# Attention scores issued as two pairs of heads, with V products and jobs between the pairs

## What is computed

```
xn = layernorm(x)
Q, K, V, U = silu(xn @ Wq), silu(xn @ Wk), silu(xn @ Wv), xn @ Wu      # 8 heads of 16
scores = (Q K^T + bias[relative position, head]) / sqrt(16), causal mask
weights = silu(scores)                                                 # no softmax
x = x + (weights @ V) * silu(U)
xn = layernorm(x)
gates = softmax over the top 2 of 8 logits (xn @ w_gate.T)
x = x + sum over e of gates[:, e] * ((xn @ w_in[e].T) @ w_out[e].T)
```

## Time and profile before

| | |
|---|---|
| median of 3 runs | 421.82 us (419.15 to 422.48) |
| profiled execution, first to last instruction (the only time shown of it) | 420.7 us |
| TensorE matmul busy | 368.3 us, 88% |
| DVE, ACT, POOL busy | 262.4, 244.1, 150.3 us |
| mean clock granted to TensorE | 0.885 of full speed |

### The profile page before, as it was taken

How to read it: one execution, slowest core, us unless ns; L and a number is a source line. 1 busy time by engine, 2 the same in 40 slices (tenths; PEclk the granted TensorE clock), 3 DMA queues, 4 the chain that set the end, 5 groups by cost and what they waited for, 6 DMA issues and landing times.

```text
span 420.7 us, 5792 instructions
## 1 busy us (share of the span) xinstructions
PE 368.3 (88%) x1708; PEld 155.3 (37%) x1708; DVE 262.4 (62%) x774; ACT 244.1 (58%) x485; POOL 150.3 (36%) x213
## 2 busy tenths in 40 slices
PE   0778869999999799999899899999999699998392
PEld 0433335455433333524333344432433243333151
DVE  3325730473887825868477539538999249568867
ACT  1426744788886557866466478845665467674013
POOL 5210220121208811446007534307527331443826
PEclk9996985999999958999569889959999779999877
DMA  4869583035602730272004700460005600000001
GB/s 76 278 212 266 161 222 95 19 101 168 158 2 57 208 87 0 62 212 54 26 2 128 197 26 0 147 179 2 26 1 170 156 26 0 2 2 25 1 0 50
DMA packets 34454, 37.89 MB, mean 90 GB/s; under 512 B 6256, under 2 KB 20080, under 8 KB 34424
## 3 DMA queue, kind: packets, MB, share of 16 engines
q1 hardware_dynamic: 34424, 37.53, 32.4%
HBM read 24.92 MB, written 12.60 MB: 89 GB/s over the span
## 4 chain that ended last, share of the span: by engine, by line
PE 59%; DMA 14%; DVE 12%; SPq 5%; POOL 4%; ACT 3%; issue 3%; DVEq 0%; POOLq 0%; ACTq 0%
PE score L555 19%; PE o_acc L571 13%; PE jobp L639 10%; DMA rows_dram<-k_hi 9%; PE jobp L599 5%; DVE score L804 4%; DMA k_stack<-rows_dram 4%; SPq L364 3%; PE jobp L594 3%; DVE xn L840 3%; ACT wts L699 2%; PE jobp L657 2%; POOL ymix L519 2%; PE jobp L632 2%; PE jobp L606 2%
## 5 line engine op out<-in xcount | busy, mean ns | idle before, releaser
L699 ACT ACTIVATE wts<-score,far 128x512 f32<-128x512 f32 (+3 forms) x384 | 201.6, 584 | 93.6 <-DVE score L804 63.4
L804 DVE TENSOR_TENSOR score<-score,bias_near 128x384 f32<-128x384 f32 (+2 forms) x320 | 128.0, 439 | 85.6 <-PE score L555 84.4
L555 PE MATMUL score<-q_stack,k_stack 64*128 64x512 f32 (+3 forms) x384 | 133.3, 469 | 22.8 <-DMA k_stack<-rows_dram 14.8
L555 PEld LDWEIGHTS score<-q_stack,k_stack 64*128 64x128 f32 x384 | 57.5, 199 | 166.5 <-issue 106.5
L519 POOL TENSOR_TENSOR ymix<-ymix 128x512 f32<-128x512 f32 (+2 forms) x84 | 69.0, 822 | 95.4 <-DVE ymix L910 90.9
L571 PE MATMUL o_acc<-wts,v_pad 128*32 128x512 f32 (+3 forms) x768 | 89.9, 543 | 1.0 <-ACT wts L699 1.0
L639 PE MATMUL jobp<-mm_e,xn2T 128*128 128x512 f32 x116 | 70.7, 702 | 0.9 <-DVE ymix L910 0.8
L910 DVE TENSOR_TENSOR ymix<-jobp,gates 128x512 f32<-128x512 f32 x56 | 38.0, 684 | 20.8 <-PE jobp L639 20.7
L594 PE MATMUL jobp<-ident,xn 128*128 128x128 f32 x64 | 13.8, 353 | 18.0 <-DVE xn L840 18.0
L840 DVE TENSOR_SCALAR xn<-xs,mv,rstd 128x128 f32<-128x128 f32 x64 | 28.0, 500 | 0.6 <-POOL rstd L458 0.4
L488 POOL TENSOR_TENSOR q_lo<-q,q_hi 128x512 fp32r<-128x512 f32 x7 | 9.7, 1393 | 50.9 <-DVE q_hi L850 50.9
(11 more groups left out here) (85 smaller groups left out, 265.4 us busy)
## 6 DMA issues: line engine op xcount, KB each, us to landing
q_stack<-rows_dram SPq DMA_DIRECT2D x64, 128.0 KB, 3.5
k_stack<-rows_dram SPq DMA_DIRECT2D x64, 128.0 KB, 3.2
rows_dram<-k_hi SPq DMA_DIRECT2D x16, 256.0 KB
xs<-in_L_attn_x SPq DMA_DIRECT2D x8, 256.0 KB, 5.3
win_s<-in_L_ffn_w_in SPq DMA_DIRECT2D x8, 256.0 KB, 2.9
wout_s<-in_L_ffn_w_out SPq DMA_DIRECT2D x8, 256.0 KB, 3.2
rows_dram<-q_hi SPq DMA_DIRECT2D x8, 256.0 KB
rows_dram<-q_lo SPq DMA_DIRECT2D x8, 256.0 KB
```

The costliest lines, as they stand in the source:

```text
L555: pe.matmul(score[j][:, 0:n], k_stack[rows, b % 2, h // 2, kb * P:(kb + 1) * P], q_stack[rows, half, h // 2, q0 - half * HALF:q0 - half * ...
L699: act.activation(wts[:, number % 2, j, 0:n], score[j][:, 0:n], ACT.Silu, bias=far[:, h:h + 1], scale=HD ** -0.5).then_inc(weighed[j], 1)
L804: dve.tensor_tensor(score[j][:, 0:near], score[j][:, 0:near], bias_near[:, 4 * quad + j, c0:c0 + near], ALU.add).then_inc(biased[j], 1)
```

## The change

TensorE now issues S0 and S1 of group i+1, then V of group i−1, then all jobs of slot i, then S2 and S3. Behind those stand S0 and S1 of group i+2, from the next slot. ACT does all jobs of slot i−1 between weigh 1 and weigh 2. DVE does add 0 and add 1 of group i+1, then the side jobs of slot i−1, then drains all banked jobs of slot i, then add 2 and add 3. A banked job that stood second in its slot is thus drained by DVE one slot sooner. No operation is added or removed, and the plan, the buffers and the waits are the same.

```diff
+def bank_jobs(jobs):
+    return [j for j in jobs if j[0] in BANKED]
+
+def side_jobs(jobs):
+    return [j for j in jobs if j[0] not in BANKED]
...
 # TensorE
                 if group and after:
                     scores(after, 0)
+                    scores(after, 1)
                 if before:
                     times_v(before)
-                if group and after:
-                    scores(after, 1)
-                for job in first_job(jobs):
+                for job in jobs:
                     job_pe(job)
                 if group and after:
                     scores(after, 2)
-                for job in later_jobs(jobs):
-                    job_pe(job)
-                if group and after:
                     scores(after, 3)
...
 # ScalarE
                 if group:
                     weigh(group, 0)
-                if i > 0 and TIMELINE[i - 1][0]:
-                    for job in first_job(TIMELINE[i - 1][1]):
-                        job_act(job)
-                if group:
                     weigh(group, 1)
                 if i > 0 and TIMELINE[i - 1][0]:
-                    for job in later_jobs(TIMELINE[i - 1][1]):
+                    for job in TIMELINE[i - 1][1]:
                         job_act(job)
                 if group:
                     weigh(group, 2)
...
 # VectorE
                 if not group:
                     if before:
-                        for job in later_jobs(TIMELINE[i - 1][1]):
+                        for job in side_jobs(TIMELINE[i - 1][1]):
                             job_dve(job)
                         copy_outputs(before)
...
                 if after:
                     add_bias(after, 0)
+                    add_bias(after, 1)
                 if group and before:
-                    for job in later_jobs(TIMELINE[i - 1][1]):
+                    for job in side_jobs(TIMELINE[i - 1][1]):
                         job_dve(job)
-                if after:
-                    add_bias(after, 1)
                 if group:
-                    for job in first_job(jobs):
+                    for job in bank_jobs(jobs):
                         job_dve(job)
                 if after:
                     add_bias(after, 2)
```

## The result

The changed kernel takes 394.81 us (median of 4 runs, 392.04 to 397.37), the kernel before 422.15 us (4 runs, 419.15 to 425.09): ratio 0.9423, 95% interval 0.9292 to 0.9554. Medians are of all runs and ratios of fast runs alone, so a ratio can differ by a per cent from the quotient of two medians. The forecast was 407, range 396 to 422 from a median of 421.8. The time moved the way that was forecast, by 27 us (24 by the ratio) instead of 15.

The account below looks back on a forecast made before the run. TensorE was taken to bound five stretches of 280.3 us, with 140.4 us fixed. Span 420.7 − 32.1 (TensorE) + 7.7 (loop) + 9.8 (DVE) = 406.1, so 407 us; range 396 to 422.

Parts of the forecast that it names:

- TensorE's slot: Full-clock slots of two banked jobs: four scores together at 0.66 and touching jobs save 0.73 us each, 16.1 over 22.
- second count, by mode changes: Two-job slots on TensorE: three tiling-mode changes instead of six at 0.22 us each give 0.66 instead of 0.73.
- Two-job slots at half clock: Ten slots of two banked jobs at half clock gain 1.0 us each on TensorE, 10 us.
- One-job slots: Twenty slots with one job of about 1 us go from 3.14 to 2.80, gaining 0.3 each, 6 us.
- The loop of V behind S1: V queued behind S1 makes a loop of 2.80 us, costing 5.0 in slots without banked job, 2.7 with short ones.
- DVE's side jobs: Side jobs on DVE between add 1 and the drains cost 9.8 us: 6.3 for nine norms, 3.5 for 35 others.
- The sum: Whole span: 420.7 − 32.1 + 7.7 + 9.8 = 406.1 us, so a time of 407; forecast case 403 to 413, chance 0.45.
- DVE hides all: Rival: DVE's side jobs cost nothing, 9.8 us less, 397 us (396 to 403); chance 0.17.
- The clock rival: Rival: 15 us more at half clock behind DMA waits, or four scores costing 0.99: 413 to 421 us; chance 0.24.
- The slower rival: Rival: side jobs make DVE last, delaying drains, adds 2 and 3 and four weighs: 432 us (426 and more); chance 0.14.
- ACT's move: ACT's jobs moved to one place between weigh 1 and weigh 2: hidden under V's 0.99, up to 0.3 us showing with V of 128 columns.
- DMA stretches: Four stretches of DRAM write and stack reload stay near 17 us each, 66.8 in all, with longer waits for the stack.

Follow-up runs that it names:

- the pairs apart: Changed kernel with TensorE's later jobs moved behind S2 and S3, and DVE draining them behind add 3: 396.97 us against 424.69.
- the spare buffer: Changed kernel with a third wts buffer for heads 0 and 1: 383.93 us against 420.12, ratio 0.9205.
- the warm version: Changed kernel with 4 idle matmuls ahead of S0 of the second unit in batches 1 to 3: 385.96 us against 423.45, ratio 0.9134.

## Why the prediction was right, and its size not

- **TensorE's slot.** Right: four scores at 0.66, jobs at 0.96, 3.57 for 3.65. In the 19 two-job slots at full clock in both profiles the gain is 0.71 us each, V to V, for 0.73; the 22 and 22 of the table give 14.5 us for 16.1. Touching jobs were taken at 0.10 less and give 0.21 (2.12 to 1.91). The prediction's second count, by mode changes, came out at 0.66 because it left out that a lone score now runs beside another. An estimate from the rows here: a second pair of scores adds 0.23 (0.66 less 0.43) and a second touching job 0.86 (1.91 less 1.05), so about 0.20 is left each time (0.43 less 0.23, 1.05 less 0.86) for the change to the next kind of work. With V, scores and jobs as the kinds, the FF slot has six such changes before, five with the pairs apart and three now. One change and one lone score less are 0.20 + 0.23 = 0.43, two more changes less are 0.40; measured were 0.42 and 0.39. One price per change thus covers both the places of the scores and the jobs that touch.
- **Two-job slots at half clock.** Mis-sized: 10 us, and by the table 30.3 less 14.5 is 15.8. They were priced as if the half-clock parts stayed; of the eight slots at half or part half clock before, three are at full clock after, and three others have fallen, so this row mixes the order with the clock.
- **One-job slots.** Mis-sized: 6 us of gain, measured a loss of 1.0. The term took the 3.14 us of a 512-query slot with a full job for all; the 18 took 2.84 before already, which is the new loop's 2.80.
- **The loop of V behind S1.** Right in kind (more waiting for V, 1.19 from V to weigh 0), too large in size: 5.0 us for slots without a job (3.3 measured) and 2.7 for short jobs (0.7). Of the 3.3 us only 0.8 lies in the eight slots at full clock in both profiles (2.21 to 2.31); 2.5 us lie in four slots that one profile has at half clock.
- **DVE's side jobs.** The term that failed most: 9.8 us of cost (its own numbers give 0.8 a norm, not 0.7). In two-job slots none of it is seen (0.82 us gained with side jobs, 0.65 without); elsewhere it was not measured by itself. DVE has less slack, though: its wait for scores fell from 84.4 to 51.6 us, and its adds have 6% of the chain instead of 4%.
- **The sum.** The case that came is the rival "DVE hides all", 397, which had 0.17, and not the forecast's own 403 to 413. That the sum without DVE's term, 397.4, is so near the 397.5 is in part luck: the two-job slots gave 4 us more than the sum has, one-job slots 7 less, the loop cost 4 less, and the DMA stretches gave 2.6 that it has at nothing.
- **The clock rival.** It had the wrong sign. It held that longer waits for the DMA would bring 15 us more at half clock; there were 19 us less in the means, worth 6 to 7 of the 27 us. It also read all four parts at half clock behind the DMA waits as over 10 us; the one behind the third is 6.8. Why the clock stays up better with the new order is not settled. Among the versions with TensorE's new order and no idle matmuls, those in which TensorE is idle less have less half clock: its short idle times (up to 1.5 us) sum in the traces to 29.9 us with its order alone, 25.1 with ACT's, 20.1 with DVE's, 13.0 in the changed kernel and 11.6 with the spare buffer, with 108, 99, 94, 81 and 61 us at half clock. The kernel before doesn't fit in: 7.6 us idle, and 101 at half clock.
- **The slower rival.** What it described, four weighs late together, was not seen: ACT's wait for the adds fell from 63.4 to 54.9 us. A case that was missed lies beside it: without the orders of ACT and DVE, TensorE's new order gives no gain that shows. The prediction put ACT's move at nothing, but without it the rest is −8.1 instead of −19.9.
- **DMA stretches.** Right: 16.1 to 16.7 us, with waits of 21.3 us for 14.8. Ahead of the low halves at 125.72 us in the chain stand DVE's adds and the high halves now, no longer POOL's sums.

## What to carry to other kernels

Matmuls of one tiling should stand together. Here a place cost 0.43 us with one or two scores of 512 columns and 0.66 with three or four, at full clock, so that each change from one kind of work to another is worth about 0.20 us (an estimate from these rows). When work is regrouped on one engine, the engines that feed and drain it must cut their queues at the same points, or what one gains the others take back. And where one program alone varies by 7% with the clock, compare the cost of the same slots at full clock, and the time at half clock apart from it, before believing a difference of a few us.

## What was not expected of the hardware

- With idle matmuls in three waits of about 4 us the granted clock behind them was 1.00, and the time 9 us less (395 to 386 us; 2.2% less in the kernel before).
- The same program had a mean clock of 0.841 to 0.918 and times of 409.8 to 438.8 us from run to run, near one line of 0.38 us for each us at half clock. In the changed kernel's profile the clock fell to half at 104.8 us for 10 us, though TensorE had been busy 25.24 of the 26 us up to 104; the warm version, which is the same program up to there, kept 1.00. Stretches of the changed kernel, then the same one of the warm version:

```profile
78.00:104.00 26.00, 25.24 (x166) 12.55 (x164) 16.02 (x50) 22.64 (x47) 5.02 (x7) 1.00 0.48 145
104.80:115.00 10.20, 10.05 (x46) 4.24 (x46) 7.24 (x27) 6.14 (x15) 0.39 (x1) 0.50 0.23 54
```

```profile
104.80:115.00 10.20, 10.00 (x60) 4.20 (x52) 9.41 (x37) 9.16 (x21) 0.00 (x0) 1.00 0.13 27
```

- A norm of four times 128x128 on DVE took 1.11 us in one place and 2.13 in another. In the second POOL summed experts at the same time (197.18 to 199.80 us), in the first it had no work; no run moved the one away from the other.
